# A mixture-of-experts kernel: roots computed earlier at the end of the attention phase, one pause per eight scatters, tile counts by a table, seven early expert tiles

## The chip, the cores and the metric

The kernel runs on one core of a Trainium2 chip. Its engines are TensorE (PE: matmuls and transposes into PSUM), VectorE (DVE), ScalarE (ACT), GpSimd (POOL, which also issues the indirect DMAs) and SyncE (SP, which issues the plain DMAs). Each runs its own instruction list in order; they wait for each other by semaphores. The metric is the device time of one execution in microseconds, the median over several runs. The profile is of one execution; its times count from that execution's first instruction.

## What is computed

Two layers on an image batch of 4 x 48 x 48 tokens of 64 channels: windowed attention and a mixture of eight experts of which each token takes two. Cut to what matters:

```python
x = x + attention(layernorm(x))        # windows of 64 tokens, 8 heads of 8, rope, mask, softmax, projection
t = x.reshape(4, 48 * 48, 64)
flat = layernorm(t).reshape(-1, 64)    # 9216 tokens
probs = softmax(flat @ router_w.T)     # 8 experts
topk_probs, topk_idx = top_k(probs, 2)
topk_probs = topk_probs / (sum(topk_probs) + 1e-09)
gates = einsum('nk,nke->ne', topk_probs, one_hot(topk_idx, 8))
h = silu(flat @ w1[e].T) * (flat @ w3[e].T)     # 682 hidden columns, for each expert e
y = h @ w2[e].T
t = t + sum over e of gates[:, e] * y
```

The outputs in float32. The kernel computes the experts only for the rows that chose them.

## The kernel before

**Attention phase.** 9,216 tokens are 72 tiles of 128, worked in 18 groups of four (G = 4). `groups` (line 289) calls an engine's `body(b)` for each group start b = 0, 4, ..., and four more times at the end to drain; a body works on five groups at once: `b` is normalized, `att_g = b - 4` has its softmax, `out_g = b - 8` its output projection, `route = b - 12` its router, `send = b - 16` its rows sent to the experts. TILES is 72, so in the drain b = TILES sends group 14, b = TILES + G group 15, and so on to group 17.

**Root.** Each layer norm needs the variance to the power -1/2. VectorE makes the variance (`ln2_variance`, line 855), GpSimd takes the power (`root`, line 1216), ScalarE multiplies (`normalize2`, line 679). The second norm of a group stands before its router logits, these before the choice of experts.

**Sending.** Each token row of 64 floats plus gate and token number (264 bytes) is written to a region of DRAM per expert. GpSimd issues one indirect DMA per 128 rows (`scatter`, line 1222; eight per group, lines 1225 and 1226). In the drain it waits with `pause` (line 1233) until scatters have landed. The last four groups have row buffers of their own.

**Counts.** When all groups are counted, VectorE works out on 128x8 numbers, in sixteen instructions (lines 1076 to 1106), where each expert's rows end (`padrow`), how many tiles of SLOTS = 384 rows each expert has left, and a running sum (`ends`) that serves as loop bounds for all engines. The division by 384 is a shift by 7, then a multiplication by 171 and a shift by 9. SyncE then writes 384 padding rows behind each expert's end (`pad_end`, line 369) in two sets of four.

**Expert phase.** One tile is 384 rows of one expert. SyncE loads it (lines 382, 383, later 402, 403), TensorE turns it (`turn_rows`), multiplies six chunks of hidden columns (`hidden`, lines 504 to 510), ScalarE does silu, VectorE the product, TensorE the down projection (`down`, line 518) and turns the result back (`turn_y`, line 528). VectorE multiplies by the gates, GpSimd adds 128 rows at a time to the output in DRAM by an accumulating indirect DMA. TensorE's third chunk of tile n waits until VectorE has emptied the result of tile n - 2 (lines 493 to 497).

**Early tiles.** Before the counts are known, the first `EARLY` tiles are worked from rows that are surely there: experts (1, 1, 1, 0, 0, 0). For the first OWN = 3 of them VectorE writes to buffers of their own (`tail_early`, line 1138) and GpSimd adds them with `add_early` (line 1299), behind all its scatters. All others go through one buffer `y_out` (`tail`, line 1147, `send_mid`, line 1128) and `add_rows` (line 1308), and the buffer is filled again only after the add of the tile before has landed (`s_added`). When the expert changes, and behind the last `add_early`, GpSimd waits for all landings first, because two adds to one output row must not overlap (lines 1318 to 1332).

**Start.** SyncE loads the first activations, then the constants `kf`, then the query weights; VectorE waits for both (lines 978, 979).

## Time and profile before

| | us |
|---|---|
| median of 3 timed runs | 697.98 |
| lowest and highest of them | 696.06, 703.49 |
| profiled execution, device time | 693.54 |
| profiled execution, span from first to last instruction | 691.2 |

In the profiled execution the busy times are PE 593.7 us (86% of the span), VectorE 484.2 (70%), GpSimd 440.0 (64%), ScalarE 414.2 (60%). The page sums up the execution: busy times, the span in 40 slices with the granted clock of TensorE, the chain of work that ended last, and groups of instructions by source line. The chain is followed back from the last instruction, at each step to what released it. A timeline row gives start, duration, engine, line, operation and, in brackets, the idle time before it and what ended that. Line numbers are those of the kernel before. "issue" means that nothing in the profile was waited for.

### The profile page before, as it was taken

How to read it: one execution, taken by the hardware profiler on the slowest of the kernel's cores; microseconds unless marked ns; L12 is line 12 of the kernel's file. 1: busy time of each engine (PE TensorE's matmuls, PEld its weight loads, DVE VectorE, ACT ScalarE, POOL GpSimd, SP SyncE). 2: the span in 40 equal slices, each digit the busy share in tenths (PEclk: the TensorE clock that was granted, in tenths of full speed). 3: DMA queues.
4: the chain of work that ended last, by engine and by line, in shares of the span. 5: the costliest groups of instructions: out<-in, count | busy, mean ns of one | idle time of the engine just before them, and what ended most of it. 6: DMA issues, size and time to landing. Idle time of an engine off the chain costs nothing.

```text
span 691.2 us, 20144 instructions
## 1 busy us (share of the span) xinstructions
PE 593.7 (86%) x5359; PEld 368.5 (53%) x5359; DVE 484.2 (70%) x1692; ACT 414.2 (60%) x934; POOL 440.0 (64%) x398
## 2 busy tenths in 40 slices
PE   1888888888888888852889999999999999999991
PEld 0466566656665556542445555555555555555550
DVE  2578878888878767763556667777676777776772
ACT  1678777778767767641345556555565565565560
POOL 1111777767767766546557876775766868666776
PEclk9999999999999999965599999999999999999996
DMA  9900000100000000001143444444434434344342
GB/s 328 295 10 9 26 27 25 33 25 25 25 24 25 24 23 24 26 25 37 45 85 39 53 43 44 50 41 48 50 38 50 44 43 52 38 50 48 38 52 16
DMA packets 85590, 34.67 MB, mean 50 GB/s; under 512 B 81966, under 2 KB 82478, under 8 KB 85038
## 3 DMA queue, kind: packets, MB, share of 16 engines
q0 software_dynamic: 26640, 9.90, 15.0%
q1 hardware_dynamic: 58910, 24.30, 14.3%
q8 instruction: 17, 0.28, 0.2%
q14 instruction: 23, 0.19, 0.1%
HBM read 20.21 MB, written 13.76 MB: 49 GB/s over the span
## 4 chain that ended last, share of the span: by engine, by line
PE 51%; issue 7%; DMA 5%; POOL 5%; DVE 4%; POOLq 1%; ACT 1%; DVEq 0%; ACTq 0%
PE bank L504 21%; PE bank L518 13%; POOL expert_rows L1225 3%; PE bank L473 3%; DMA expert_rows<-rows,slot_u 3%; PE bank L451 2%; PE bank L509 2%; PE bank L441 2%; PE bank L463 2%; PE bank L634 2%; DMA out<-y_early,meta 1%; PE bank L528 1%; DMA out<-y_out,token 1%; DVE smax L960 1%; PE bank L435 1%
## 5 line engine op out<-in xcount | busy, mean ns | idle before, releaser
L1313 POOL DMA_INDIRECT out<-y_out,token x144 | 222.8, 1547 | 89.2 <-DVE y_out L1136 53.1
L1225 POOL DMA_INDIRECT expert_rows<-rows,slot_u x144 | 147.8, 1027 | 79.2 <-issue 27.5
L504 PE MATMUL bank<-xs,w_sb 64*128 64x384 f32 x510 | 182.2, 500 | 4.7 <-DVE hid L1175 1.8
L505 PE MATMUL bank<-xs,w_sb 64*128 64x384 f32 x510 | 182.5, 501 | 0.0
L779 ACT ACTIVATE gate_h<-bank 128x384 f32<-128x384 f32 x255 | 125.2, 492 | 61.2 <-PE bank L505 43.6
L1175 DVE TENSOR_TENSOR hid<-gate_h,bank 128x384 f32<-128x384 f32 x255 | 140.4, 554 | 30.2 <-ACT gate_h L779 13.2
L504 PEld LDWEIGHTS bank<-xs,w_sb 64*128 64x128 f32 x510 | 92.0, 189 | 88.2 <-issue 39.4
L518 PE MATMUL bank<-hid,w_sb 128*64 128x384 f32 x612 | 110.5, 496 | 2.7 <-DVE hid L1175 2.7
L505 PEld LDWEIGHTS bank<-xs,w_sb 64*128 64x128 f32 x510 | 92.0, 189 | 0.0
L789 ACT ACTIVATE y_odd<-bank 64x384 f32<-64x384 f32 x51 | 24.9, 487 | 85.9 <-PE bank L518 82.0
L1168 DVE TENSOR_TENSOR y_t<-y_odd,bank 64x384 f32<-64x384 f32 x51 | 27.8, 546 | 56.3 <-ACT y_odd L789 53.4
L518 PEld LDWEIGHTS bank<-hid,w_sb 128*64 128x64 f32 x612 | 40.6, 136 | 47.3 <-issue 42.4
L463 PE MATMUL bank<-v_bd,pt 128*64 128x18 f32 x1152 | 48.4, 217 | 20.3 <-ACT pt L693 17.4
L693 ACT ACTIVATE pt<-bank 128x512 f32<-128x512 f32 x72 | 42.8, 595 | 38.2 <-PE bank L451 34.3
L463 PEld LDWEIGHTS bank<-v_bd,pt 128*64 128x64 f32 x1152 | 42.0, 142 | 36.3 <-issue 35.8
L1220 POOL TENSOR_TENSOR ln_rstd<-ln_vare,minus_half 128x4 f32<-128x4 f32 x36 | 37.5, 1042 | 33.1 <-issue 22.3
L698 ACT ACTIVATE probs<-probs 128x512 f32<-128x512 f32 x72 | 45.2, 627 | 21.8 <-DVE probs L963 21.8
L960 DVE TENSOR_REDUCE smax<-bank 128x8 f32<-128x512 f32 x72 | 49.1, 681 | 6.0 <-PE bank L441 3.8
L743 ACT ACTIVATE k_bd<-bank,consts 128x512 f32<-128x512 f32 x72 | 43.6, 689 | 14.8 <-PE bank L608 14.7
L963 DVE TENSOR_TENSOR probs<-bank,smax 128x512 f32<-128x512 f32 x72 | 49.8, 691 | 3.0
L451 PE MATMUL bank<-consts,probs 128*128 128x128 f32 x288 | 49.6, 297 | 2.2 <-ACT probs L698 1.5
L451 PEld LDWEIGHTS bank<-consts,probs 128*128 128x128 f32 x288 | 31.9, 147 | 23.7 <-issue 22.6
(136 smaller groups left out, 977.2 us busy)
## 6 DMA issues: line engine op xcount, KB each, us to landing
xin<-expert_rows SPq DMA_DIRECT2D x51, 99.0 KB
xin<-expert_rows SPq DMA_DIRECT2D x51, 96.0 KB
w_sb<-w SPq DMA_DIRECT2D x1, 3072.0 KB, 22.1
out<-res_all SPq DMA_DIRECT2D x18, 128.0 KB
expert_rows<-rows,slot_u POOLq DMA_INDIRECT x144
out<-y_out,token POOLq DMA_INDIRECT x144
x_all<-x_win SPq DMA_DIRECT2D x1, 1664.0 KB, 8.6
res_all<-x_res SPq DMA_DIRECT2D x1, 1664.0 KB, 12.1
```

Source lines behind the costliest of these rows:

```text
L451: mm = pe.transpose(ps_pt[:, pr * P:(pr + 1) * P], probs[:, jt % 2, 2 * pr:2 * pr + 2, :], ident)
L463: mm = pe.matmul(ps_pv[w * N:(w + 1) * N, jt * 72 + pr * 18:jt * 72 + (pr + 1) * 18], pt[:, jt % 2, pr, w * N:(w + 1) * N], v_bd[:, jt, w, ...
L504: pe.matmul(ps_h[c % RING], w13_sb[0:C, e, c, :], xs[0:C, :], start=True, stop=True)
L505: pe.matmul(ps_g[c % RING], w13_sb[C:2 * C, e, c, :], xs[C:2 * C, :], start=True, stop=True).then_inc(s_h, 1)
L518: mm = pe.matmul(ps_y[half * C:(half + 1) * C, :], w2_sb[:, e, c, :], hid[:, c, :], start=(c < 2), stop=(c >= CHUNKS - 2))
L698: act.activation(probs[:, jt % 2, :, :], probs[:, jt % 2, :, :], ACT.Exp).then_inc(s_exp, 1)
L779: mm = act.activation(gate_h[:, c % RING, :], ps_h[c % RING], ACT.Silu)
L960: dve.reduce_max(top_s, sc, AX).then_inc(s_max, 1)
L963: dve.tensor_tensor(probs[:, jt % 2, :, :].rearrange("p (x h) k -> p x h k", x=2), sc, top_s.unsqueeze(3).to_broadcast([P, 2, HEADS // 2, ...
L1175: mm = dve.tensor_tensor(hid[:, c, :], gate_h[:, c % RING, :], ps_g[c % RING], ALU.mult)
L1225: pool.indirect_dma_start(rows_dram, bass.IndirectOffsetOnAxis(ap=slot_u[:, spar, i // 2, i % 2:i % 2 + 1], axis=0), rows[:, spar, i // 2, ...
L1313: pool.indirect_dma_start(out, bass.IndirectOffsetOnAxis(ap=token[:, c:c + 1], axis=0), y_out[:, c, :], None, compute_op=ALU.add).then_inc ...
```

## The change

It touches six places.

1. **Roots.** In the drain, GpSimd computed the root of group 16 between scatters 6 and 7 of group 14, and that of group 17 between scatters 6 and 7 of group 15. Now both stand in group 14's body: group 16's behind its second scatter, group 17's behind its eighth.
2. **Pauses.** Before, GpSimd waited after the fourth and after the eighth scatter of each drained group. Now it waits after the eighth, and not at all in group 14.
3. **Counts.** A table of 24 tile ends per expert stands in the constants. One comparison of 128x8x24 and one sum give the number of tiles left; the shifts and the multiplication go. Sixteen instructions become eight.
4. **Early tiles.** `EARLY` gets a fourth tile of expert 0, and the first four early tiles have buffers and adds of their own. Each tile comes out as before, 51 in all.
5. **Constants.** `kf` grows from 422 to 606 columns of 128 x 4 bytes.
6. **Regions.** The longest skip grows by 384 rows, so all regions in DRAM do, and one more padding write of 384 rows is issued at the start.

The partner sum of the keys (line 608) stands ahead of the output projection (line 614) in both kernels; the diff has nothing on it.

```diff
-EARLY = (1, 1, 1, 0, 0, 0)
-OWN = 3
+EARLY = (1, 1, 1, 0, 0, 0, 0)
+OWN = 4
...
-K_COLS = 422
+K_COLS = 414 + E * MOST
...
             dve.wait_ge(s_cnt, 1)
-            dve.tensor_copy(cnt_f[:], ps_cnt).then_inc(s_tstep, 1)
+            dve.tensor_tensor(padrow_f[:], ps_cnt, late_base[:], ALU.add).then_inc(s_tstep, 1)
             dve.wait_ge(s_tstep, 1)
...
+            dve.tensor_tensor(over[:], padrow_f[:].unsqueeze(2).to_broadcast([P, E, MOST]), tile_ends, ALU.is_gt).then_inc(s_tstep, 1)
+            dve.tensor_copy(padrow_i[:], padrow_f[:])
             dve.wait_ge(s_tstep, 2)
...
+            dve.reduce_sum(til_m[:], over[:], AX).then_inc(s_tstep, 1)
...
                     hold(pool)
-                    scatter(to, (0, 1, 2, 3), par)
-                    pause(send, par, 4)
-                    scatter(to, (4, 5), par)
-                    if ok(out_g):
+                    scatter(to, (0, 1), par)
+                    if b == TILES:
                         root(ln2_rstd, ln2_vare, s2vare, s2rstd, s2xn, out_g)
-                    scatter(to, (6, 7), par)
-                    pause(send, par, 8)
+                    scatter(to, range(2, 2 * G), par)
+                    if b == TILES:
+                        root(ln2_rstd, ln2_vare, s2vare, s2rstd, s2xn, out_g + G)
+                    else:
+                        pause(send, par, 2 * G)
...
-    kf[:, K_TIL:K_TIL + E] = np.arange(E) * REGION + np.array(SKIP) - (SLOTS - 1)
+    ends = (np.arange(E) * REGION + np.array(SKIP))[:, None] + np.arange(MOST)[None, :] * SLOTS
+    ends[:, 0] = -1
+    kf[:, K_ENDS:K_ENDS + E * MOST] = ends.reshape(-1)
```

GpSimd's instructions from the last group's body to the ordinary adds, before; `ln_rstd` is a root, `expert_rows` a scatter, `y_early` an early add and `y_out` an ordinary one:

```order
L1225 DMA expert_rows<-rows,slot_u 86016x66 x6
L1220 TENSOR_TENSOR ln_rstd<-ln_vare,minus_half 128x4
L1225 DMA expert_rows<-rows,slot_u 86016x66 x8
L1220 TENSOR_TENSOR ln_rstd<-ln_vare,minus_half 128x4
L1225 DMA expert_rows<-rows,slot_u 86016x66 x8
L1220 TENSOR_TENSOR ln_rstd<-ln_vare,minus_half 128x4
L1225 DMA expert_rows<-rows,slot_u 86016x66 x18
L1305 DMA out<-y_early,meta 9600x64 x9
L1313 DMA out<-y_out,token 9600x64 x9
```

And of the changed kernel:

```order
L1204 DMA expert_rows<-rows,slot_u 89088x66 x6
L1199 TENSOR_TENSOR ln_rstd<-ln_vare,minus_half 128x4
L1204 DMA expert_rows<-rows,slot_u 89088x66 x4
L1199 TENSOR_TENSOR ln_rstd<-ln_vare,minus_half 128x4
L1204 DMA expert_rows<-rows,slot_u 89088x66 x6
L1199 TENSOR_TENSOR ln_rstd<-ln_vare,minus_half 128x4
L1204 DMA expert_rows<-rows,slot_u 89088x66 x24
L1285 DMA out<-y_early,meta 9600x64 x12
L1293 DMA out<-y_out,token 9600x64 x9
```

Of the roots the first is group 15's, which stays; group 16's moves up by four scatters, group 17's by six. Twenty-four scatters follow the last root where eighteen did, and three early adds are new.

VectorE's counts, between the metadata of the last group and the first tile, before (the first ten of sixteen):

```order
L1076 COPY cnt_f<-bank 128x8
L1078 TENSOR_TENSOR padrow_f<-cnt_f,late_base 128x8
L1080 TENSOR_TENSOR til_f<-padrow_f,consts 128x8
L1082 CAST til_i<-til_f 128x8
L1083 CAST padrow_i<-padrow_f 128x8
L1085 TENSOR_SCALAR til_s<-til_i 128x8
L1088 CAST til_f<-til_s 128x8
L1090 TENSOR_SCALAR til_m<-til_f 128x8
L1092 CAST til_i<-til_m 128x8
L1094 TENSOR_SCALAR til_s<-til_i 128x8
```

And the whole of it in the changed kernel:

```order
L1072 TENSOR_TENSOR padrow_f<-bank,late_base 128x8
L1075 TENSOR_TENSOR over<-padrow_f,consts 128x192
L1076 CAST padrow_i<-padrow_f 128x8
L1078 TENSOR_REDUCE til_m<-over 128x8
L1080 SCALAR_TENSOR_TENSOR ends_f<-til_m,zero 128x8
L1082 TENSOR_SCALAR ends_mf<-ends_f 128x8
L1084 CAST ends_m<-ends_mf 128x8
L1085 CAST ends_i<-ends_f 128x8
```

The chain is half as long; the comparison `over` is 192 columns wide.

## Rows read from the trace of the kernel before

**Rows 1.** The page: granted TensorE clock in 40 slices, tenths of full speed.

```profile
PEclk9999999999999999965599999999999999999996
```

**Rows 2.** Chain of work that ended last: start us, us, what.

```profile
326.87 2.20 DMA expert_rows<-rows,slot_u
...
355.09 3.38 DMA expert_rows<-rows,slot_u
...
359.39 3.49 DMA out<-y_early,meta
...
374.30 3.18 DMA out<-y_early,meta
378.30 3.28 DMA out<-y_out,token
385.67 2.09 PE bank L518 x12
392.15 2.09 PE bank L518 x12
```

**Rows 3.** Timeline of GpSimd (POOL): start us, us, what [idle before <-releaser].

```profile
301.25 0.97 POOL L1225 DMA_INDIRECT expert_rows<-rows,slot_u  x1 [2.25 <-issue]
...
309.16 1.04 POOL L1220 TENSOR_TENSOR ln_rstd<-ln_vare,minus_half 128x4 f32<-128x4 f32 x1
...
324.29 1.04 POOL L1220 TENSOR_TENSOR ln_rstd<-ln_vare,minus_half 128x4 f32<-128x4 f32 x1
...
329.99 0.96 POOL L1225 DMA_INDIRECT expert_rows<-rows,slot_u  x1 [2.16 <-DMA expert_rows<-rows,slot_u]
331.25 0.96 POOL L1225 DMA_INDIRECT expert_rows<-rows,slot_u  x1 [0.30 <-issue]
```

**Rows 4.** Timeline of TensorE (PE).

```profile
330.25 0.98 PE L504 MATMUL bank<-xs,w_sb 64*128 64x384 f32 x1 [0.67 <-ACT xs L702]
...
338.83 0.97 PE L504 MATMUL bank<-xs,w_sb 64*128 64x384 f32 x1 [1.84 <-DVE hid L1175]
...
382.11 0.56 PE L504 MATMUL bank<-xs,w_sb 64*128 64x384 f32 x1 [0.36 <-DVE y_out L1162]
```

**Rows 5.** Timelines of VectorE (DVE) and, one row, ScalarE (ACT).

```profile
6.18 1.11 DVE L982 COPY v_bd<-consts 128x8 f32<-128x8 f32 x8 [0.17 <-DMA wqkv_sb<-w_qkv]
...
303.39 0.20 DVE L858 TENSOR_SCALAR ln_vare<-ln_var 128x4 f32<-128x4 f32 x1
...
317.33 0.17 DVE L858 TENSOR_SCALAR ln_vare<-ln_var 128x4 f32<-128x4 f32 x1
...
335.08 0.16 DVE L1076 COPY cnt_f<-bank 128x8 f32<-128x8 f32 x1
...
338.14 1.94 DVE L1175 TENSOR_TENSOR hid<-gate_h,bank 128x384 f32<-128x384 f32 x4
...
351.68 0.36 DVE L1145 TENSOR_TENSOR y_early<-bank,meta 128x192 f32<-128x192 f32 x1
...
381.67 0.17 DVE L1160 COPY token<-meta 128x2 uint16<-128x2 uint16 x1 [2.52 <-DMA out<-y_out,token]
...
310.24 1.06 ACT L686 ACTIVATE xn<-ln_c,ln_rstd 128x64 f32<-128x64 f32 x4
```

**Rows 6.** Windows of 1 us: busy us of each engine, PEclk, DMA share, GB/s.

```profile
342.00:343.00 1.00, 1.00 (x5) 0.49 (x6) 0.43 (x2) 0.49 (x1) 0.00 (x0) 0.60 0.10 34
...
678.00:679.00 1.00, 0.06 (x1) 0.00 (x0) 0.27 (x2) 0.00 (x0) 0.70 (x2) 1.00 0.00 0
...
680.00:681.00 1.00, 0.00 (x0) 0.00 (x0) 0.35 (x2) 0.00 (x0) 0.69 (x2) 0.86 0.03 8
```

**Rows 7.** The queue of SyncE (SPq), and a window of the start.

```profile
344.44 5.26 SPq L371 DMA_DIRECT2D expert_rows<-pad_sb  x4
...
354.04 4.46 SPq L371 DMA_DIRECT2D expert_rows<-pad_sb  x4
...
4.00:5.00 1.00, 0.00 (x0) 0.00 (x0) 0.00 (x0) 0.00 (x0) 0.00 (x0) 1.00 1.00 369
```

More of the change, by code:

```diff
@@ L71 @@
 BIG = -1.0e30
-THIRD, THIRD_SHIFT = 171, 9
-assert SUB == 3 and all(x * THIRD >> THIRD_SHIFT == x // SUB for x in range(TOKENS // P + SUB + 1))
+MOST = TOKENS // SLOTS
+assert MOST * SLOTS == TOKENS
 MASKED_PER_IMAGE = PER_IMAGE // 3
@@ L90 @@
 FIRST_TILES = 5 * G
-K_IDENT, K_ROPE, K_SUM, K_HEAD, K_VMASK, K_IOTA, K_BASE, K_SKIP, K_TIL = 0, 128, 256, 384, 388, 390, 398, 406, 414
-K_COLS = 422
+K_IDENT, K_ROPE, K_SUM, K_HEAD, K_VMASK, K_IOTA, K_BASE, K_SKIP, K_ENDS = 0, 128, 256, 384, 388, 390, 398, 406, 414
+K_COLS = 414 + E * MOST
 W_QK, W_V, W_BIAS, W_VBIAS = 0, 128, 192, 194
@@ L132, in build @@
         early_rows = consts[:, K_SKIP:K_SKIP + E]
-        tile_base = consts[:, K_TIL:K_TIL + E]
+        tile_ends = consts[:, K_ENDS:K_ENDS + E * MOST].rearrange("p (e t) -> p e t", e=E)
         ident_b = constb[:, B_IDENT:B_IDENT + P]
@@ L189, in build @@
         late_base = sb("late_base", [P, E])
-        cnt_f = sb("cnt_f", [P, E])
-        cnt_i = sb("cnt_i", [P, E], I32)
-        til_i = sb("til_i", [P, E], I32)
-        til_s = sb("til_s", [P, E], I32)
-        til_f = sb("til_f", [P, E])
+        over = sb("over", [P, E, MOST])
         til_m = sb("til_m", [P, E])
@@ L1075, in _ @@
             dve.wait_ge(s_cnt, 1)
-            dve.tensor_copy(cnt_f[:], ps_cnt).then_inc(s_tstep, 1)
+            dve.tensor_tensor(padrow_f[:], ps_cnt, late_base[:], ALU.add).then_inc(s_tstep, 1)
             dve.wait_ge(s_tstep, 1)
-            dve.tensor_tensor(padrow_f[:], cnt_f[:], late_base[:], ALU.add).then_inc(s_tstep, 1)
+            dve.tensor_tensor(over[:], padrow_f[:].unsqueeze(2).to_broadcast([P, E, MOST]), tile_ends, ALU.is_gt).then_inc(s_tstep, 1)
+            dve.tensor_copy(padrow_i[:], padrow_f[:])
@@ L1079, in _ @@
             dve.wait_ge(s_tstep, 2)
-            dve.tensor_tensor(til_f[:], padrow_f[:], tile_base, ALU.subtract).then_inc(s_tstep, 1)
+            dve.reduce_sum(til_m[:], over[:], AX).then_inc(s_tstep, 1)
             dve.wait_ge(s_tstep, 3)
-            dve.tensor_copy(til_i[:], til_f[:]).then_inc(s_tstep, 1)
-            dve.tensor_copy(padrow_i[:], padrow_f[:]).then_inc(s_tstep, 1)
+            dve.tensor_tensor_scan(ends_f[:], til_m[:], zero8[:], float(len(EARLY)), ALU.add, ALU.add).then_inc(s_tstep, 1)
@@ L1084, in _ @@
+            dve.wait_ge(s_tstep, 4)
+            dve.tensor_scalar(ends_mf[:], ends_f[:], float(-BEHIND), None, ALU.add).then_inc(s_tstep, 1)
             dve.wait_ge(s_tstep, 5)
-            dve.tensor_scalar(til_s[:], til_i[:], P.bit_length() - 1, None, ALU.arith_shift_right).then_inc(s_tstep, 1)
-            dve.wait_ge(s_tstep, 6)
-            dve.tensor_copy(til_f[:], til_s[:]).then_inc(s_tstep, 1)
-            dve.wait_ge(s_tstep, 7)
-            dve.tensor_scalar(til_m[:], til_f[:], float(THIRD), None, ALU.mult).then_inc(s_tstep, 1)
@@ L1101, in _ @@
-            dve.tensor_tensor_scan(ends_f[:], til_m[:], zero8[:], float(len(EARLY)), ALU.add, ALU.add).then_inc(s_tstep, 1)
-            dve.wait_ge(s_tstep, 13)
-            dve.tensor_scalar(ends_mf[:], ends_f[:], float(-BEHIND), None, ALU.add).then_inc(s_tstep, 1)
-            dve.wait_ge(s_tstep, 14)
             dve.tensor_copy(ends_m[:], ends_mf[:])
```

9 lines of the change are left out of this document (removed).

## Prediction

> **What bounds the kernel now.** I read the clock line of the page first, then the chain of work that ended last in order of time, then the timelines of the engines that this chain names. The clock line shows a dent in slices 18 to 20 of 40 [rows 1]. It is the passage from the attention groups to the expert tiles, some 298 to 382 us, and nearly the whole diff lies in it. Behind it the chain is TensorE's: the down projections of consecutive tiles start at 385.67 and 392.15, one tile per 6.49 us [rows 2]. So a microsecond taken from the passage is one of the span, if it is taken from what ends last there.
>
> What ends last there is GpSimd. The chain goes through its scatters, through the landings that its pauses wait for and through nine early adds, and ends with the landing of the first ordinary add (378.30 + 3.28), which releases VectorE's copy of the token numbers at 381.67 [rows 2, 5]. VectorE had waited 2.52 us for it; TensorE's third chunk of tile 6 (counted from 0) waits for VectorE until 382.11, but only 0.36 us [rows 4]. TensorE's own stream and GpSimd's arrive at nearly the same moment today.
>
> The first expert tile hangs on two other waits: on the root of the last group, which GpSimd computes at 324.29 though its input was ready at 317.33 + 0.17, and on VectorE's chain of counts, 335.08 to 338.14, behind which TensorE resumes at 338.83 after 1.84 us [rows 3 to 5].
>
> **Early roots.** The root of group 16 runs at 309.16 on an input that ends at 303.39 + 0.20 [rows 3, 5]. Now it stands behind the second scatter, which ends at 301.25 + 0.97, so it runs at 303.6 to 304.7. Group 16's normalization gains nothing to speak of: ScalarE does it at 310.24 right behind the copy of group 17's turned attention [rows 5]. Six scatters follow, from 304.9, one per 1.26 us (329.99 to 331.25) [rows 3]; they end at 312.2. Then GpSimd stands for five microseconds at the root of group 17, whose input comes at 317.50, and ends it at 318.65. This root comes 6.7 us earlier, and the expert stream of TensorE with it. Queued behind it on GpSimd are all scatters of group 15: with 0.9 us from a release to the first scatter (329.99 - 326.87 - 2.20) they begin at 319.55 [rows 2, 3].
>
> **One pause per eight.** A group had two pauses, a step of 3.12 us each (326.87 to 329.99) where a plain step takes 1.26. With one it takes seven plain steps, 8.8 us, and one of 3.12, 11.9 in place of 13.8. Beside the padding rows a pause is longer; the last one, up to the first early add, took 4.30 (355.09 to 359.39) [rows 2, 3]. The padding is released by the counts and moves with them, from 344.44 and 354.04 to 336.4 and 346.0, still among the scatters [rows 7]. For the second and third pause I take 3.7, between 3.12 and 4.30, since half of their neighbourhood is padding. Group 15: 319.55, last scatter 328.4. Group 16: 331.5, last 340.3. Group 17: 344.0, last 352.8. First early add 356.5 against 359.39: 2.9 us earlier. With 3.12 for all pauses it is 4.0, with 4.30 twice 1.7.
>
> The landing in such a pause is 2.20 us in a quiet place and 3.38 beside padding [rows 2]. The Trainium skill ("DMA: Bandwidth & Descriptors", section "Anatomy of one DMA") puts one transfer issued from GpSimd at 2.0 us plus its bytes over 436 GB/s, whatever else runs: an estimate of 2.08 us for the 33.8 KB of a scatter. By that GpSimd would be another 1.5 us earlier and the sum below 0.95 us faster than before instead of 0.55 slower. The trace agrees in the quiet place only, so I stay with the rows.
>
> **Seven early tiles, four with adds of their own.** There are 51 tiles as before: expert 0 has 2,042 of its 2,617 rows by group 13, more than four tiles of 384. On GpSimd three adds are new, and one wait: tile 3 belongs to another expert than tile 2 and its adds wait for all landings of tiles 0 to 2, and the first ordinary add waits for landings again. From the last add before such a wait to the next add pass 4.00 us (374.30 to 378.30), between adds 1.86 (359.39 to 374.30 in eight steps) [rows 2]. New in front of the first ordinary add: 4.00 + 2 x 1.86 = 7.7 us. It comes at 378.30 - 2.9 + 7.7 = 383.1, 4.8 us later. It now belongs to tile 4, so TensorE waits for it in tile 7, one tile later, which is worth 6.49 us. Tile 7's third chunk starts at 382.11 + 4.8 = 386.9, against 382.11 + 6.49 = 388.6 before: **1.7 us gained**, 2.8 and 0.5 at the two bounds of the pauses. VectorE's product for an early tile takes 0.36 us and hides where its three steps for an ordinary one did [rows 5].
>
> **Counts by a table.** Sixteen small instructions in 3.06 us become eight. Six are of the old kind at 0.2 us each or less; the comparison and the sum over 192 columns cost 0.36 each by the product of 128x192, and at most 0.55 by a product of 128x384 [rows 5]. That makes 1.7 us, 1.35 gained on the way to tile 0. With the root, the expert stream of TensorE starts 8.05 us earlier. All of it runs into the wait for the first ordinary add: tile 7's third chunk could start at 388.6 - 8.05 - 0.36 = 380.2 and starts at 386.9.
>
> **What this wait does to the clock.** TensorE then stands for some 6.7 us in the middle of its full speed. In this trace its last products at full clock are in 678 to 679, and within 680 to 681 the granted clock falls to half (1.2 of 2.4 GHz); resuming at 338.83 after the 1.84 us idle it ran at half until within 342 to 343 [rows 4, 6]. So I count 4.0 us at half clock, of which half is lost: **2.0 us**. The lower bound is nothing (no fall). The upper bound takes tile 0's whole time at half clock, from its first product at 330.25 to 342.6, 12.3 us less 1.84 idle, half of it 5.2 [rows 4, 6].
>
> The Trainium skill ("TensorE: Matmul & The Clock Gate", section "HAM oscillation") tells of waits after which each burst starts cold again; its figure for a burst is 1.67 us at half clock, 0.8 lost, with which the sum would be 0.65 us faster than before. The trace agrees that the clock falls, and shows a longer stretch.
>
> **The table's load.** The constants grow by 184 columns, 94 KB, ahead of the query weights, whose landing is the last thing that VectorE's first work on the constants waits for (6.18 us, 0.17 waited) [rows 5]; at the 369 GB/s of that stretch this is **0.25 us**, all on the path [rows 7]. A seventh padding write at the start lies under the load of the expert weights; uncovered it would cost as much.
>
> **Sum.** -1.7 + 2.0 + 0.25 = +0.55 us on the profiled run of 693.54 (span 691.2). The median of the three timed runs, 697.98, is 4.4 above the profiled one, and they lie 7.4 apart. I put the same difference on the median: **698.5 us**, no change that can be told.
>
> **Rivals.**
> *The clock holds* (0.17): -1.45, 696.5 us. For it: at the end of the program it held for about two microseconds of idle. Against it: the wait here is three times that.
> *The expert stream keeps its 8 us* (0.06), what the change looks like at first sight. For that the first ordinary add would have to come by 375, 8 us before my 383.1; the time would be 697.98 - 8.05 - 0.36 + 0.25 = 689.8. Against it: adds and scatters follow each other without a gap and only 2.9 us of pauses go.
> *Longer at half clock* (0.14): 5.2 us in place of 2.0, +3.75, 701.7 us. For it: all of tile 0 ran at half. Against it: behind this wait TensorE has nothing more to wait for.
> *Eight scatters without a pause drain more slowly* (0.08), the one that ends slower: if landings fall behind by 0.3 us per scatter, each of the three pauses is 2.4 us longer, +7.2 + 0.55, 705.7 us; from 0.27 us on it is slower by over 1%. Against it: the landing of a fourth scatter, 2.20, shows no backlog [rows 2].
> The likeliest (0.55) is that the first ordinary add decides and the clock falls for some 4 us.
>
> **Chances and range.** About 1%, 7 us, is what a measurement of this kernel can tell from no change. Faster by more: the second rival and a share of the runs' own scatter, 0.07. Slower by more: the last rival and such a share, 0.09. Between: 0.84. The likeliest with its bounds gives -2.8 + 0 + 0.25 to -0.5 + 5.2 + 0.25, 695.4 to 702.9; the scatter of the runs widens it to 693 to 704, which leaves out less than 2 in 10.
>
> **What would show it.** Right: group 17's root on GpSimd at 317.6, tile 0's first product near 323.5, the early adds from 356.5, the first ordinary add at 383.1, TensorE idle for 6 to 7 us in tile 7 while VectorE waits for an add, and a granted clock of 0.50 behind it for some 4 us. Wrong: no long idle in tile 7, steps between scatters over 1.26 us, or a late first ordinary add without TensorE waiting for it.

## The result and the profile after

| | us |
|---|---|
| kernel before, median of 20 runs beside the changed kernel | 698.44 (691.69 to 705.71) |
| changed kernel, median of 20 runs | 701.98 (695.79 to 708.79) |
| ratio changed / before | 1.007, 95% interval 1.004 to 1.010 |
| changed kernel, profiled execution | 700.72 (span 698.9) |
| the same two kernels on two other occasions: ratio | 0.999 (0.995 to 1.003) and 0.996 (0.993 to 0.999) |

The forecast was 698.5 us and no change that can be told (the prediction took 7 us for the least that can be). That holds: the three ratios lie on both sides of 1, each within 0.7% of it, and the first differs from the other two by more than their intervals. But the way to it was another than forecast, as the passage from the attention groups to the expert tiles shows. The page's clock line, granted TensorE clock in 40 slices, stands against [rows 1]:

```profile
PEclk9999889999999999965689999999999999999997
```

There is a shallow dent in slices 5 and 6, in attention work that the change does not touch; it comes back below. The dent of the passage is in slices 18 to 20 as before, and a weak one follows in slice 21.

**GpSimd went as forecast up to the first early add.** Timeline of GpSimd in the changed kernel: start us, us, what, idle before it and what ended that. It answers to [rows 3].

```profile
309.77 1.04 POOL L1199 TENSOR_TENSOR ln_rstd<-ln_vare,minus_half 128x4 f32<-128x4 f32 x1 [2.37 <-issue]
...
323.51 1.04 POOL L1199 TENSOR_TENSOR ln_rstd<-ln_vare,minus_half 128x4 f32<-128x4 f32 x1 [5.14 <-issue]
...
332.42 0.96 POOL L1204 DMA_INDIRECT expert_rows<-rows,slot_u  x1 [0.30 <-issue]
333.68 0.96 POOL L1204 DMA_INDIRECT expert_rows<-rows,slot_u  x1 [0.30 <-issue]
336.80 0.96 POOL L1204 DMA_INDIRECT expert_rows<-rows,slot_u  x1 [2.16 <-issue]
...
345.65 0.96 POOL L1204 DMA_INDIRECT expert_rows<-rows,slot_u  x1 [0.30 <-issue]
349.23 0.96 POOL L1204 DMA_INDIRECT expert_rows<-rows,slot_u  x1 [2.62 <-DMA expert_rows<-rows,slot_u]
...
358.08 0.96 POOL L1204 DMA_INDIRECT expert_rows<-rows,slot_u  x1 [0.31 <-issue]
361.19 1.60 POOL L1285 DMA_INDIRECT out<-y_early,meta  x1 [2.15 <-issue]
...
368.14 1.55 POOL L1285 DMA_INDIRECT out<-y_early,meta  x1 [1.60 <-DVE y_early L1124]
...
376.10 1.55 POOL L1285 DMA_INDIRECT out<-y_early,meta  x1 [2.71 <-DVE y_early L1124]
...
383.83 1.55 POOL L1285 DMA_INDIRECT out<-y_early,meta  x1 [2.47 <-DMA out<-y_early,meta]
...
391.79 1.55 POOL L1293 DMA_INDIRECT out<-y_out,token  x1 [2.71 <-DMA out<-y_early,meta]
```

The whole drain starts 5.19 us later in this execution than in the one of before: VectorE's `filled`, the first step of it, stands at 300.15 against 294.96. All times of the passage are compared less that. The early root of group 17 then stands at 318.3 (forecast 317.6) and the first early add at 356.0 (forecast 356.5). Eight scatters in a row keep their 1.26 us each, and their pauses take 3.12, 3.58 and 3.11 us.

**TensorE's stream lost its lead in tiles 0 to 2.** Chain of the work that ended last in the changed kernel: start us, us, what. It answers to [rows 2].

```profile
330.63 5.58 another core or an unknown queue
336.80 0.94 PE bank L500
...
348.30 1.54 issue
...
352.36 2.61 another core or an unknown queue
354.99 0.49 ACT xs L698
355.48 5.25 another core or an unknown queue
360.80 0.50 ACT y_odd L785
361.39 0.56 DVE y_t L1147
362.08 0.97 PE bank L500
```

In before this chain had run through GpSimd's scatters and pauses. Now it runs through waits of 5.58, 2.61 and 5.25 us that no instruction of the trace accounts for. The rows of VectorE, ScalarE and TensorE say what was waited for:

```profile
336.29 0.19 DVE L909 TENSOR_TENSOR place<-bank,late_base 128x32 f32<-128x32 f32 x1 [5.51 <-remote]
```

```profile
348.56 0.49 ACT L785 ACTIVATE y_odd<-bank 64x384 f32<-64x384 f32 x1 [2.62 <-remote]
...
360.80 0.49 ACT L785 ACTIVATE y_odd<-bank 64x384 f32<-64x384 f32 x1 [5.33 <-remote]
```

```profile
332.47 0.19 PE L572 MATMUL bank<-counted,constb 128*128 128x32 bf16 x1
336.62 0.17 PE L636 MATMUL bank<-counted,constb 128*128 128x8 bf16 x1 [3.97 <-DVE counted L910]
...
343.74 2.42 PE L514 MATMUL bank<-hid,w_sb 128*64 128x384 f32 x12
352.28 2.16 PE L514 MATMUL bank<-hid,w_sb 128*64 128x384 f32 x12
362.08 0.97 PE L500 MATMUL bank<-xs,w_sb 64*128 64x384 f32 x1 [4.26 <-DVE y_t L1147]
366.70 2.88 PE L514 MATMUL bank<-hid,w_sb 128*64 128x384 f32 x12
```

Each late step reads a TensorE product. `place` reads the product of 332.47, done at 332.66, and starts at 336.29. `y_odd` of tile 1 reads the down projection of 352.28, done at 354.44, and starts at 360.80. The records of the semaphores say the same. A down projection sends three increments, which in an undisturbed tile come 0.02 us behind the modelled end of its thirds. For the projection of 352.28 they came at 357.81, 360.67 and 360.73, the last 6.3 us late; for that of 343.74 at 348.36, 348.42 and 348.48, in one bunch. So TensorE's products stood in the trace as ended while their readers still waited. The Trainium skill ("Perfetto Trace Analysis", section "Tensor Engine Instruction (MATMUL, LD_WEIGHTS)") says that a matmul's end in a profile is estimated from its size, and that the increment is pushed only when PSUM has acknowledged the writes. The trace agrees that end and increment are two events, here up to 6.3 us apart. Whether the products or only their increments were late, no row here can tell.

Tile 2's down projection starts at 366.70, 66.55 us behind `filled`, where before it was 63.39. The stream that came out of the roots early is 3.2 us late by its third tile, and in tile 7 there is no long wait any more. VectorE's timeline of the changed kernel:

```profile
395.01 0.17 DVE L1139 COPY token<-meta 128x2 uint16<-128x2 uint16 x1 [0.30 <-DMA out<-y_out,token]
```

### The profile page after: what moved, and what is told of

The parts are those of the page before. It is cut to its first block, busy times and chain, and to the rows that moved or that the text cites. A ratio compares the mean times of both kernels' runs of the same rounds, so it can differ in the third digit from the quotient of the medians.

```text
span 698.9 us, 20076 instructions
## 1 busy us (share of the span) xinstructions
PE 600.1 (86%) x5359; PEld 372.1 (53%) x5359; DVE 482.2 (69%) x1678; ACT 414.5 (59%) x934; POOL 439.5 (63%) x398
## 3 DMA queue, kind: packets, MB, share of 16 engines
HBM read 20.31 MB, written 13.86 MB: 49 GB/s over the span
## 4 chain that ended last, share of the span: by engine, by line
PE 57%; issue 6%; DVE 5%; another core or an unknown queue 2%; ACT 2%; DMA 1%; ACTq 1%; POOL 1%; DVEq 0%; POOLq 0%
PE bank L500 24%; PE bank L514 15%; PE bank L469 3%; PE bank L447 2%; PE bank L505 2%; PE bank L437 2%; PE bank L459 2%; PE bank L630 1%; PE bank L524 1%; DVE smax L956 1%; PE bank L431 1%; PE bank L501 1%; ACT pt L689 1%; DVE k_st L966 1%
## 5 line engine op out<-in xcount | busy, mean ns | idle before, releaser
L1293 POOL DMA_INDIRECT out<-y_out,token x141 | 218.2, 1548 | 88.5 <-DVE y_out L1115 51.3
```

Source lines behind the costliest of these rows:

```text
L1293: pool.indirect_dma_start(out, bass.IndirectOffsetOnAxis(ap=token[:, c:c + 1], axis=0), y_out[:, c, :], None, compute_op=ALU.add).then_inc ...
```

## The experiments

They ran on three occasions, each on another chip, called A, B and C here. The kernel before took 695.47 (A), 686.41 (B) and 697.45 us (C) there. Executions of one kernel on one occasion lie up to 14 us apart, so the passage is read from marks of the traces as well, each counted from `filled`. Each row of marks is one trace. From `filled` to the end three traces of one kernel differ by 1.5 us (before) and 1.9 us (changed), so a difference of that size in one pair shows little.

**A: the two kernels again, pauses per four, six tiles.** The changed kernel and the kernel before, unedited:

> The changed kernel once more, with a trace of its own. In its first trace TensorE's increments reached VectorE and ScalarE late seven times between 336 and 361 us (waits of 2.2 to 5.5 us put down to an unknown queue), which cost the expert products of tiles 1 to 7 the 8 us of lead that the earlier route had given them. Theory 'burst' (eight row scatters in a row without a pause hold up TensorE's increments): the late increments come again at the same places, the first down-projection of tile 2 starts more than 20 us after that of tile 0 (66.55 - 43.59 = 23.0 in the first trace, 16.4 in the kernel before), and the ratio of times is again 1.004 to 1.010. Theory 'accident of one execution': the waits are gone, tile 2's down-projection follows tile 0's by some 16 us, the stream waits some 6 us in tile 7 for rows as predicted, and the ratio scatters about 1.

> The kernel before once more, with a trace of its own: how much its own marks move from one execution to the next. Theory 'burst': no increment of TensorE is late by over 2 us in the drain, and tile 2's down-projection follows tile 0's by 16 to 17 us again. Theory 'accident': such late increments turn up here too, at least one of over 2 us.

Pauses per four, an edit of the changed kernel:

```
-                    scatter(to, range(2, 2 * G), par)
+                    scatter(to, (2, 3), par)
+                    pause(send, par, 4)
+                    scatter(to, (4, 5, 6, 7), par)
```

> The changed kernel with the old pause after four scatters put back in the drain; the roots stay early, the counts by the table and seven expert tiles stay. Theory 'burst': the late increments vanish, tile 2's down-projection follows tile 0's by 16 to 17 us, VectorE's wait ahead of place is under 2 us (5.5 us in the changed kernel's trace), and the ratio falls to 0.99 to 1.00, while the first early add comes 2 to 4 us later. Theory 'accident': nothing changes against the changed kernel run beside it but the first early add, later by 2 to 4 us, which moves the end by less than 2 us.

Six tiles, again of the changed kernel:

```
-EARLY = (1, 1, 1, 0, 0, 0, 0)
-OWN = 4
+EARLY = (1, 1, 1, 0, 0, 0)
+OWN = 3
```

> The changed kernel with six tiles ahead of the loops as before (three early tiles and three own), all else as changed: the first ordinary add comes some 7.7 us earlier relative to the first early add (27 instead of 35 us... in the traces 18.9 us before the change and 30.6 us after it), so that whatever waits on y_out has these microseconds less to wait. Theory 'the seventh tile costs': the span from the start of the drain falls by 2 us or more (ratio 0.995 to 1.000). Theory 'burst' and theory 'accident' alike: it does not move the end (ratio within 0.003 of the changed kernel's), because the late increments of TensorE, or nothing, decide the start of the stream.

(The first sentence of that expectation starts with two figures that are no measurements, 27 and 35; those behind them, 18.9 and 30.6 us, are the ones of the traces. And the first expectation of A counts seven late increments from 336 to 361 us; the rows have five waits of 2.2 to 5.5 us.)

| marks, us behind `filled` | tile 0 down | tile 2 down | from 0 to 2 | first early add | first ordinary add | tile 10 down | to the end |
|---|---|---|---|---|---|---|---|
| before | 47.04 | 63.39 | 16.35 | 64.43 | 83.34 | 116.86 | 396.24 |
| before again (A) | 47.16 | 61.82 | 14.66 | 64.39 | 83.17 | 117.06 | 396.64 |
| changed | 43.59 | 66.55 | 22.96 | 61.04 | 91.64 | 119.75 | 398.75 |
| changed again (A) | 41.02 | 64.36 | 23.34 | 59.26 | 89.61 | 118.15 | 397.47 |
| pauses per four (A) | 37.08 | 52.46 | 15.38 | 65.38 | 92.12 | 120.75 | 400.00 |
| six tiles (A) | 40.09 | 64.54 | 24.45 | 59.26 | 81.78 | 117.10 | 395.91 |

Ratios to before on A: changed 0.999 (0.995 to 1.003), pauses per four 1.006 (1.003 to 1.010), six tiles 0.998 (0.994 to 1.001).

The late increments are no accident of one execution. With bursts of eight tile 2 follows tile 0 by 23.0 to 24.5 us, with four by 14.7 to 16.4, in two kernels each. The waits view (waits for which the releaser is unknown: total us, times, longest) for the changed kernel again, then for pauses per four, then for before again:

```profile
ACT y_odd L785 <- remote: 6.7, 1, 6.7
DVE place L909 <- remote: 4.6, 1, 4.6
ACT pt L689 <- remote: 1.6, 1, 1.6
```

```profile
ACT y_odd L785 <- remote: 5.7, 2, 3.2
ACT pt L689 <- remote: 1.6, 1, 1.6
```

```profile
ACT pt L693 <- remote: 1.5, 1, 1.5
```

The kernel before is not free of it either: in its first trace three increments of one tile's products with L504 came in one bunch, at 349.30, 349.36 and 349.42, and in its second trace the longest delay in tiles 0 to 2 is 1.2 us. More than that: the records of the semaphores show late increments of TensorE in both kernels all through the attention phase (the last section has the counts). The change did not bring them, it let them grow.

Not all came as expected. The marks of the changed kernel came again, its ratio did not (0.999 for 1.004 to 1.010). With pauses per four the first early add came 6.1 us later, not 2 to 4, and increments came up to 2.2 us late. With six tiles the end came 1.6 us sooner, under the 2 us named for 'the seventh tile costs', and the ratio lies within 0.003 of the changed kernel's, as the other theories had it. My expectation that with pauses per four the ratio would fall was wrong too: it rose. That run shows why. The stream kept its lead, and then the step of the prediction came true which the changed kernel itself had skipped. TensorE in tile 7, pauses per four:

```profile
376.57 0.48 PE L501 MATMUL bank<-xs,w_sb 64*128 64x384 f32 x1
388.57 0.98 PE L500 MATMUL bank<-xs,w_sb 64*128 64x384 f32 x1 [11.51 <-DVE y_out L1141]
...
391.94 0.84 PE L501 MATMUL bank<-xs,w_sb 64*128 64x384 f32 x1
392.54 0.50 PE L505 MATMUL bank<-xs,w_sb 64*128 64x192 f32 x1
```

VectorE ahead of it:

```profile
388.13 0.17 DVE L1139 COPY token<-meta 128x2 uint16<-128x2 uint16 x1 [13.70 <-DMA out<-y_out,token]
```

And the windows of this kernel (window, its length, busy time and instructions of PE, PEld, DVE, ACT and POOL, granted clock, DMA share, GB/s):

```profile
382.00:388.00 6.00, 0.00 (x0) 0.00 (x0) 0.00 (x0) 0.00 (x0) 3.30 (x3) 0.50 0.20 11
388.00:393.00 5.00, 4.43 (x16) 2.83 (x17) 3.25 (x11) 1.10 (x3) 4.08 (x4) 0.51 0.35 22
393.00:399.00 6.00, 6.00 (x42) 3.27 (x40) 3.78 (x12) 3.42 (x8) 3.96 (x3) 1.00 0.47 52
```

TensorE waits 11.5 us for the first ordinary add, its clock is at 1.2 of 2.4 GHz when it resumes, and stays there from 388.57 to 392.54, 4.0 us. Late increments or not, tile 7 cannot pass before GpSimd's add; with four more pauses that add is 2.5 us later than in the changed kernel beside it, and so is the end.

**B: one part alone, pad stores later, pauses per two.** The early roots with bursts of eight in the kernel before (its old counts and six tiles kept) is the drain of the change:

```
-                    scatter(to, (0, 1, 2, 3), par)
-                    pause(send, par, 4)
-                    scatter(to, (4, 5), par)
-                    if ok(out_g):
+                    scatter(to, (0, 1), par)
+                    if b == TILES:
                         root(ln2_rstd, ln2_vare, s2vare, s2rstd, s2xn, out_g)
-                    scatter(to, (6, 7), par)
-                    pause(send, par, 8)
+                    scatter(to, range(2, 2 * G), par)
+                    if b == TILES:
+                        root(ln2_rstd, ln2_vare, s2vare, s2rstd, s2xn, out_g + G)
+                    else:
+                        pause(send, par, 2 * G)
```

> The kernel before with the drain's order alone changed (both roots early, scatters in bursts of eight); counts and tile numbers as before. Theory 'burst': late increments as in the changed kernel (tile 2's down-projection 22 to 25 us behind tile 0's), the first ordinary add at about 82 to 83 us behind the start of the drain, and the span from there within 1.5 us of the 396.2 to 396.6 of the kernel before: what the early roots give is taken by the bursts. If the late increments need the new counts, tile 2 follows by 16 us and the span falls to about 392.

The table of counts alone: the changed kernel with this piece and the tile numbers put back.

> The kernel before with the table of counts alone (which also makes the constants' load larger); roots, pauses and tile numbers as before. By the prediction's terms the chain of the counts gives 1.35 us and the load takes 0.25 us: the step from padrow to the tile counts takes 1.8 us instead of 3.1, but tile 2's pads and loads lie behind the scatters, so the span from the start of the drain falls by 0 to 1.4 us (394.9 to 396.6). Tile 2's down-projection follows tile 0's by 15 to 17 us as before.

The stores of the pad rows later, in the changed kernel with six tiles:

```
-                if n == 2:
+                if n == 4:
                     sp.wait_ge(s_tile, 2)
-                if n in (2, 3):
+                if n in (4, 5):
                     for k in range(E // 2):
-                        pad_end((n - 2) * (E // 2) + k)
+                        pad_end((n - 4) * (E // 2) + k)
```

> The changed kernel with six tiles, and with SyncE's eight stores of pad rows issued two tiles later (four behind the load of tile 4 and four behind that of tile 5, instead of tiles 2 and 3), so that none of them overlaps the row scatters. In the six-tile kernel's trace TensorE's increments for the down-projections of tiles 0 and 1 came 3.5 and 4.9 us late, with a scatter burst and a pad store both under way. Theory 'scatters alone': the increments stay late by 3 us or more in both tiles, tile 2's down-projection follows tile 0's by 22 us or more (24.5 in the six-tile kernel), and the span from the start of the drain stays within 1.5 us of 395.9. Theory 'pad stores': the increments are late by under 1.5 us, tile 2 follows tile 0 by 16 to 19 us, and that span falls to 390 to 393 us. Theory 'both add': in between, 19 to 22 us.

A pause behind every second scatter, with six tiles:

```
-                    scatter(to, range(2, 2 * G), par)
+                    pause(send, par, 2)
+                    scatter(to, (2, 3), par)
+                    pause(send, par, 4)
+                    scatter(to, (4, 5), par)
+                    pause(send, par, 6)
+                    scatter(to, (6, 7), par)
```

> The changed kernel with six tiles and with a pause after every two scatters of the drain. If the length of a burst sets how late TensorE's increments come, tile 2's down-projection follows tile 0's by 15 to 17 us (24.5 with bursts of eight, 15.4 with bursts of four), no increment is late by over 1.5 us, and the first early add comes some 10 us later than with bursts of four (75 us behind the start of the drain instead of 65), so that tile 6 waits for its rows' buffer by 10 us or more and the span from the start of the drain is over 400 us. If only the scatters' number counts, tile 2 still follows by over 20 us.

| marks, us behind `filled` | tile 0 down | from 0 to 2 | first early add | first ordinary add | tile 10 down | to the end | ratio |
|---|---|---|---|---|---|---|---|
| roots and bursts alone | 39.51 | 14.19 | 60.75 | 79.63 | 114.07 | 394.22 | 0.995 (0.994 to 0.997) |
| table of counts alone | 45.89 | 13.86 | 65.78 | 85.03 | 119.37 | 398.72 | 0.998 (0.996 to 1.000) |
| six tiles, pads later | 38.95 | 14.04 | 61.19 | 81.07 | 115.87 | 395.49 | 0.990 (0.987 to 0.992) |
| six tiles, pause per two | 40.49 | 14.92 | 80.44 | 99.18 | 134.99 | 414.61 | one execution, 702.84 us |

These runs overturned a part of my theory. With bursts of eight in the kernel before I had expected 22 to 25 us between tiles 0 and 2 and an end within 1.5 us of 396.2; it was 14.19 and 394.22. With the table alone I had expected the end at 394.9 to 396.6; it was 398.72, though the ratio is below 1. The kernel before has no trace on B, so the marks of B compare with each other and not with a trace of it. On B no wait for an unknown releaser stands in any of the four traces, and no down projection's last increment is late by over 0.03 us, with bursts of eight either. Two tiles take 14 us there. The attention phase is shorter too: `filled` stands at 284.7 to 285.1 us, against 292.8 to 300.15 elsewhere. So bursts alone are not the cause: something of the chip or of the occasion comes in, and these runs cannot part the two. On the pads and on the length of a burst these runs say nothing. What the two edits give by themselves on B they do say: roots and bursts -0.5%, table -0.2%, the latter with an interval that reaches 1.000.

On B the stream comes early and waits. VectorE with roots and bursts alone, and below it TensorE:

```profile
367.81 0.27 DVE L1160 COPY token<-meta 128x2 uint16<-128x2 uint16 x1 [8.23 <-DMA out<-y_out,token]
```

```profile
368.25 0.98 PE L504 MATMUL bank<-xs,w_sb 64*128 64x384 f32 x1 [6.03 <-DVE y_out L1162]
```

This is the kind of wait that I had forecast, in the tile that needs the landing of the first ordinary add (tile 6, since this kernel has six early tiles), 6.0 us for the forecast 6 to 7. The pause per two shows its cost at the other end: the first early add moves from 61 to 80 us (75 expected), and all behind it with it.

**C: all of it side by side.** The changed kernel, the kernel before, six tiles, and six tiles with the pads later, each as above:

> The changed kernel a third time, beside the kernel before on the same chip. The late increments of TensorE stood in both earlier traces of it (tile 2's down-projection 23.0 and 23.3 us behind tile 0's), and in none of four kernels run on another chip, on which the kernel before takes 686.4 us, although three of them scatter as long bursts as it or shorter ones. Theory 'the chip decides': if this chip's kernel before is again near 686 us, tile 2 follows by 15 to 16 us, the lead of the stream ends in a wait ahead of tile 7 of 10 to 20 us, with TensorE's clock at 1.2 GHz after it, and the ratio is 1.000 to 1.006; if it is near 696 us, tile 2 follows by 22 us or more. Theory 'the kernel decides': 22 us or more on either chip.

> The kernel before a third time, with a trace, for its marks on the same chip as the others of this call: the span from the start of the drain 396 to 397 us if the chip is as the first two, and 396 to 400 if it is as the third, where the same body with the table of counts took 398.7 us.

> The changed kernel with six tiles once more, for a comparison with seven on a chip of whichever kind this is. Theory 'the seventh tile costs by its three adds': the first ordinary add comes 7.5 to 10 us earlier than with seven (8.9 and 9.0 us between the traces so far: 81.8 against 89.6 and 91.6), the stream's wait for it is shorter by about one tile less than that, and the span from the start of the drain is 1.5 to 3 us shorter (395.9 against 397.5 and 398.8), ratio to the seven-tile kernel 0.996 to 0.998. Where no increment is late, the stream arrives earlier and waits longer, so that the seventh tile's cost rises to 2 to 4 us.

> The changed kernel with six tiles and the pad stores two tiles later, beside the six-tile kernel without that on the same chip. On the chip of its first run no kernel had late increments, so that run said nothing on what makes them late. If this chip has them: theory 'pad stores' gives 15 to 19 us from tile 0's to tile 2's down-projection, theory 'scatters alone' 22 us or more. If this chip has none: the pad stores cost or give nothing in the burst, the loads behind them come later by one step in tile 5, and the span from the start of the drain is within 1 us of the six-tile kernel's.

| marks, us behind `filled` | tile 0 down | from 0 to 2 | first early add | first ordinary add | tile 10 down | to the end | ratio |
|---|---|---|---|---|---|---|---|
| changed | 41.42 | 23.64 | 59.78 | 90.09 | 117.56 | 396.85 | 0.996 (0.993 to 0.999) |
| before | 46.97 | 14.61 | 64.43 | 83.29 | 117.07 | 397.73 | |
| six tiles | 40.24 | 23.33 | 60.30 | 79.92 | 116.05 | 395.55 | 0.994 (0.991 to 0.998) |
| six tiles, pads later | 40.42 | 21.38 | 59.71 | 80.45 | 116.62 | 395.05 | 0.995 (0.992 to 0.999) |

Chip C is of A's kind. The kernel with late pads took 14.04 us from tile 0 to 2 on B and takes 21.38 here: not the kernel but the chip, or the occasion, decides whether increments come late at all. What the pads do is less plain. ScalarE's timeline of this kernel, whose first pad store is issued at 360.59:

```profile
340.61 0.49 ACT L785 ACTIVATE y_odd<-bank 64x384 f32<-64x384 f32 x1 [3.34 <-remote]
342.75 0.49 ACT L775 ACTIVATE gate_h<-bank 128x384 f32<-128x384 f32 x1 [1.65 <-remote]
351.14 0.49 ACT L785 ACTIVATE y_odd<-bank 64x384 f32<-64x384 f32 x1 [3.17 <-remote]
```

All three waits lie before that store and among the scatters. With the pads among them, in the six-tile kernel beside it, the waits of `y_odd` were twice as long:

```profile
343.27 0.49 ACT L785 ACTIVATE y_odd<-bank 64x384 f32<-64x384 f32 x1 [5.68 <-remote]
355.19 0.49 ACT L785 ACTIVATE y_odd<-bank 64x384 f32<-64x384 f32 x1 [6.52 <-remote]
```

By the spacing of the tiles (21.4 us against 23.3, and 14.0 on B) the pads make 2 of some 9 us. That is near the 22 us of 'scatters alone', and within the 19 to 22 us of 'both add' in the expectation on B. By the increments they make more: the last one of the down projections of tiles 0 and 1 is 1.7 and 1.5 us late here, 3.1 and 4.4 with the pads among the scatters; 'pad stores' had named under 1.5, 'scatters alone' 3 us or more. Without the pads each burst still delays many increments by about 1 us, and these add up: ScalarE's waits of 0.9 to 1.1 us ahead of the `gate_h` in tiles 1 and 2 are mostly of 0.15 us on B. So both add, with one trace on either side.

The run of the changed kernel could not part its two theories, since with 697.45 us for the kernel before both named 22 us or more; it is the one with late pads that does. Its ratio, 0.996, and the 0.999 of A agree within their intervals. The kernel before came out at 397.73 us from `filled`, 0.7 us above what had been expected for this kind of chip. Against seven tiles six moved the first ordinary add by 10.2 us and the end by 1.3 us, just outside the expected 7.5 to 10 and 1.5 to 3; their ratio, 0.998, is as expected.

## Why the prediction was right and where it was wrong

- **Root of group 17.** Forecast 6.7 us earlier; 6.0, 7.8 and 7.0 us earlier against the kernel before of the same occasion, counted from `filled`. Right.
- **One pause per eight.** Forecast: first early add 2.9 us earlier. It came 3.4, 5.1 and 4.7 us earlier. The step was sized for pauses of 3.7 us beside the pads; the first trace had 3.58 and 3.11 there. The rival by which eight scatters drain more slowly is refuted: GpSimd's steps stayed at 1.26 us and its pauses at most 0.5 us above the 3.12 of before. The prediction had a second value for that pause: the Trainium skill ("DMA: Bandwidth & Descriptors", section "Anatomy of one DMA") gives a transfer a fixed part that scales with nothing, an estimate of 2.08 us for a scatter. With the 0.9 us to the next scatter that is 3.0 us, also an estimate; the trace's 3.12, 3.58 and 3.11 us lie between it and my 3.7.
- **Counts by a table.** Forecast 1.7 us; from `padrow` at 337.85 to the first `hid` at 339.68 it is 1.83, and 1.70 on C. Right for the chain. Of the 1.35 us that it was to give at tile 0 only 0.56 shows on B, between roots and bursts alone (39.51) and the same with the table, six tiles and late pads (38.95).
- **The expert stream starts 8.05 us earlier.** Of that 3.45, 6.1 and 5.6 us arrived at tile 0's down projection, where increments come late; a part was lost in the late `place` (5.51 us, and 4.64 in the two later traces, where the kernel before waited 1.98), which holds the counts and TensorE behind them. On B, without late increments, the kernel with roots, bursts and table has tile 0 at 38.95, 6.9 us ahead of the one with the table alone; the roots were to give 6.7. Sized right; what was missing is below.
- **All of it runs into the wait for the first ordinary add. This is the step that failed.** I had every microsecond of the lead live until tile 7, because in the trace of before TensorE's products and their readers followed each other without a gap that mattered. In the changed kernel the lead was gone by tile 2: TensorE's increments came up to 6.3 us late while GpSimd scattered eight in a row. Tile 2 came 3.2, 2.5 and 3.5 us later than in the kernel before of the same occasion, not 8 us earlier. The prediction had named the sign of it, no long idle in tile 7, and that is what the trace shows. With the lead kept the step comes true: a wait of 11.5 us with pauses per four and of 6.0 us on B.
- **First ordinary add 4.8 us later.** Counted from `filled`: 8.3, 6.4 and 6.8 us later. In the first trace the stretch from the first early add to it grew by 11.7 us, not 7.7, because GpSimd waited 1.60 and 2.71 us for VectorE's rows of the tiles that were late. Against six tiles on the same chip the seventh costs 7.8 us (A, as forecast) and 10.2 us (C) at this add, and 1.6 and 1.3 us at the end.
- **2.0 us for the clock.** The clock fell, though in tile 2 and not in tile 7, behind 4.26 us of waiting. Windows of the changed kernel, columns as above:

```profile
356.00:361.00 5.00, 1.83 (x12) 0.89 (x8) 0.00 (x0) 0.20 (x1) 2.43 (x3) 1.00 0.45 101
361.00:368.00 7.00, 5.92 (x22) 3.55 (x24) 4.18 (x9) 3.50 (x8) 4.74 (x3) 0.53 0.44 47
368.00:374.00 6.00, 6.00 (x42) 3.47 (x40) 3.06 (x6) 3.32 (x7) 4.64 (x3) 0.98 0.38 45
```

  Nearly seven microseconds at 1.2 GHz, with 5.92 us of products in them. But the early root also ends the long stretch at half speed sooner. From `filled` to 110 us behind it the granted clock is at half for 44.4 us in all three traces of the kernel before and for 47.8, 47.8 and 44.4 us in those of the changed one: 1.7 us lost in two of them and nothing in the third, for the forecast 2.0. In the place for which the term was worked out, behind the wait for the add, half speed lasted 4.0 us with products, as forecast. The Trainium skill ("TensorE: Matmul & The Clock Gate", section "HAM oscillation — how this bites in real kernels") has 1.67 us for its kernel. The stretches here are longer, 4.0 us and nearly seven.
- **0.25 us for the larger constants.** Hardly to be found. VectorE's first copy behind this load, changed kernel:

```profile
6.30 0.93 DVE L978 COPY v_bd<-consts 128x8 f32<-128x8 f32 x8 [0.40 <-DMA wqkv_sb<-w_qkv]
```

  Its wait for the load is 0.23 us longer than in [rows 5], but it starts only 0.12 us later and ends 0.06 us earlier. Over three traces each it starts at 6.10 to 6.57 us against 6.07 to 6.18. What the load costs at the end is below what this shows.

**The sum.** Forecast +0.55 us. From `filled` to the end the changed kernel took 398.75, 397.47 and 396.85 us, mean 397.7, the kernel before 396.24, 396.64 and 397.73, mean 396.9: +0.8, less than either kernel's own spread. That there is no large change has a reason: until GpSimd has scattered, added its own tiles and landed the first ordinary add, the stream cannot be further than tile 6 or 7, whether TensorE spends its lead waiting there or in late increments before it. That the figure comes so near is in part luck. The gain of 1.7 us in tile 7 did not come, since the stream was late on its own: tile 7's down projection starts 2.9, 0.3 and 0.5 us later than in the kernel before. In the first trace GpSimd's adds themselves waited 4.3 us for the late tiles.

**What the first ratio adds.** 1.007 in the first measurement is +5 us. Of the 7.7 us between the two profiled spans 5.2 lie ahead of `filled`, in code that is the same but for the larger constants, the regions and one padding write. That profile of the changed kernel stood at half speed for 10.2 us in one piece from 81.5 us on (the shallow dent above), and none of the others has more than 6.8 us in one piece ahead of `filled`; in its second trace `filled` came at 296.03, in before's at 298.56. So in that pair of profiles this part was not the change. The median of 20 runs is not explained by one profile, but every run has its mean granted clock on record. For the changed kernel a run with 0.01 less of it took 5 to 6 us longer on each occasion. Its mean was 0.939 in the first measurement and 0.947 on A, so some 4 of the 5.8 us between its two medians go with the clock. That of the kernel before in the first measurement is not on record, apart from its profile, so the cause of the ratio 1.007 stays open.

**A version that is ahead of the changed kernel.** Early roots, bursts and table with six tiles instead of seven: 0.998 on A, 0.994 on C, each 0.15 to 0.2% below the changed kernel beside it, and its marks give 1.6 and 1.3 us. It is in front of the changed kernel on both chips, by less than the intervals of the ratios can prove; against the kernel before the interval excludes 1 on C alone. With the pads later it is 0.990 on B and 0.995 on C; on C, where the six-tile kernel without that edit ran beside it, the edit gave nothing.

## What to carry to other kernels

When a chain is shortened ahead of an engine that must wait for something else later, look for that later release first: its time, not the shortened chain, can set the end, and what is gained then only becomes another idle stretch, here with a fall of the clock behind it (11.5 us of waiting, then 4.0 us at 1.2 GHz). Extra work for the engine that makes the release (here three adds for a seventh early tile) can cost at the end even if it removes a wait elsewhere: 1.6 and 1.3 us in the two pairs of traces here. Compare marks counted from a common point in the traces, since a phase that was not touched can move more than the change; and before a delay is laid to the change, look for it in the kernel before and in the phases that were not touched.

## What the hardware showed that was not expected

TensorE's semaphore increments can come up to 6.3 us behind the modelled end of the product while GpSimd issues row scatters. That was so in the first measurement and on chips A and C, in all ten traces, those of the kernel before included. Call an increment late when every product with its semaphore that had ended had done so over 0.15 us before.

| TensorE's increments | before the first scatter (70 to 72 us) | from there to 4 us behind the last | behind that, to 650 us |
|---|---|---|---|
| ten traces (first, A, C): late of recorded | 0 of 63 | 85 to 105 of 279 to 302 | 0 or 1 of 405 to 435 |
| four traces (B): late of recorded | 0 of 63 | 0 of 304 to 333 | 0 of 440 to 494 |

Behind the last scatter GpSimd issues accumulating adds, and no delays go with these. Of VectorE's and ScalarE's own increments none was late in the ten traces (on B three of VectorE's in one trace, by up to 0.38 us). What the change altered is the size. The longest delay is 2.2 us in all three traces of the kernel before, with pauses per four 2.2, with late pads 2.2, and 4.4 to 6.3 us in the five traces with eight scatters in a row and the pad stores among them. So the long ones came where both were there; each of the two was taken away in one trace. Only waits for products of TensorE were concerned: `place`, `xs`, `y_odd`, `pt`, `gate_h` and once `y_early`.

On chip B no increment of TensorE was late in four kernels, one of which also ran on C and was late there. There `filled` comes 8 to 15 us sooner. A part of that is the clock, at half for 3.4 us between 20 us and `filled`, 6.8 to 20.5 us in the other ten traces; what the late increments of the attention phase make of the rest is not shown. B also differs in the record: up to 650 us its traces hold 98 to 99% of TensorE's increments, the others 88 to 91%, and lack even more of VectorE's and ScalarE's. The loss begins with the scatters but goes on behind them, where nothing is late, so it is not the missing records that make increments look late. Whether the recording has a part in the delays, what B has different, whether the late event is the increment or the product itself, and whether pauses per four help by their length or because they shift scatters against tiles, stays open. The changed kernel with seven tiles was not run on B.
